# One accumulator in place of two for the first experts' scatter-add

## What is computed

```python
# T = 4096, K = 8, E = 64, CAP = 256, H = 256, F = 128
topk_idx, topk_w = _route(x, gate_weight, e_bias)            # 8 experts of each token, with weights
...
xe = jnp.zeros((E, CAP, H)).at[sorted_e, pos].set(tok_sorted, mode='drop')
h = silu(einsum('ech,efh->ecf', xe, w1)) * einsum('ech,efh->ecf', xe, w3)
ye = einsum('ecf,ehf->ech', h, w2)
...
out = segment_sum(vals * flat_w[:, None], flat_t, num_segments=T)
return out + shared
```

## Time and profile before

| | |
|---|---|
| three runs | 5909.79, 5924.18 (median), 5935.9 us |
| profiled execution, span | 5916.1 us (nothing is shown around it) |
| PE busy | 5058.1 us, 85% |
| DVE busy | 3390.4 us, 57% |
| ACT busy | 2567.7 us, 43% |
| POOL busy | 1828.3 us, 31% |
| first experts' phases, from the first gather to the last statistics | 235.6 to 693.0 and 2048.6 to 2506.0 us |

### The profile page before, as it was taken

How to read it: one execution, slowest core, us unless ns; L and a number is a source line. 1 busy time by engine, 2 the same in 40 slices (tenths; PEclk the granted TensorE clock), 3 DMA queues, 4 the chain that set the end, 5 groups by cost and what they waited for, 6 DMA issues and landing times. The chain is left out here.

```text
span 5916.1 us, 82750 instructions
## 1 busy us (share of the span) xinstructions
PE 5058.1 (85%) x29088; PEld 2711.9 (46%) x29088; DVE 3390.4 (57%) x6345; ACT 2567.7 (43%) x5102; POOL 1828.3 (31%) x1800
## 2 busy tenths in 40 slices
PE   6566489999978566499987999999999999799996
PEld 3455333333325455357973333333333333255896
DVE  7511468887846721241119788878888878343111
ACT  2311217776662311132215176766766766513221
POOL 2388311111101288534331122222222222104332
PEclk9778779999989687699998899999999999889998
DMA  3476561222213277606986411221221221120798
GB/s 107 116 148 149 138 171 33 62 58 68 62 53 104 76 156 151 149 26 212 330 269 198 108 37 40 63 49 40 64 47 40 64 48 40 55 69 1 267 318 268
DMA packets 503528, 659.28 MB, mean 111 GB/s; under 512 B 147310, under 2 KB 358318, under 8 KB 497998
## 3 DMA queue, kind: packets, MB, share of 16 engines
q1 hardware_dynamic: 370158, 500.99, 27.0%
q0 software_dynamic: 133056, 154.15, 13.2%
HBM read 489.33 MB, written 164.20 MB: 110 GB/s over the span
## 5 line engine op out<-in xcount | busy, mean ns | idle before, releaser
L1724 DVE TENSOR_REDUCE ea_mx<-ea_psA 128x1 f32<-128x512 f32 (+3 forms) x2304 | 1373.9, 653 | 242.0 <-PE ea_psA L1585 144.1
L1706 ACT ACTIVATE ea_pr<-ea_psB 128x512 f32<-128x512 f32 (+3 forms) x2560 | 1198.9, 535 | 567.4 <-PE ea_psB L1608 557.7
L1585 PE MATMUL ea_psA<-ex_kx,ex_qx 99*128 99x512 bf16 (+3 forms) x2560 | 868.4, 357 | 20.2 <-DVE ea_mx L1724 13.3
L1608 PE MATMUL ea_psB<-ex_qx,ex_kx 99*128 99x512 bf16 (+3 forms) x2560 | 846.2, 349 | 0.0
L1724 DVE TENSOR_REDUCE ba_mx<-ba_psA 128x1 f32<-128x512 f32 (+3 forms) x1152 | 686.2, 653 | 144.3 <-PE ba_psA L1585 95.6
L1706 ACT ACTIVATE ba_pr<-ba_psB 128x512 f32<-128x512 f32 (+3 forms) x1280 | 601.5, 536 | 288.9 <-PE ba_psB L1611 155.5
L1625 PE MATMUL ea_psO<-ea_pr,ea_vx 128*32 128x512 f32 (+3 forms) x5120 | 603.5, 543 | 20.9 <-POOL ea_pr L1554 14.0
L1585 PEld LDWEIGHTS ea_psA<-ex_kx,ex_qx 99*128 99x128 bf16 x2560 | 250.3, 98 | 551.8 <-DVE ea_mx L1724 427.8
L1585 PE MATMUL ba_psA<-bx_kx,bx_qx 108*128 108x512 bf16 (+3 forms) x1280 | 443.5, 364 | 7.8 <-PEq L1146 4.5
L1608 PE MATMUL ba_psB<-bx_qx,bx_kx 108*128 108x512 bf16 (+3 forms) x1280 | 424.9, 349 | 14.6 <-DMA bx_qx<-ba_mT 14.4
L1608 PEld LDWEIGHTS ea_psB<-ex_qx,ex_kx 99*128 99x128 bf16 x2560 | 246.5, 98 | 310.3 <-ACT ea_pr L1706 141.0
(11 more groups left out here) (528 smaller groups left out, 8260.9 us busy)
## 6 DMA issues: line engine op xcount, KB each, us to landing
de_wg<-in_L_rg SPq DMA_DIRECT2D x64, 512.0 KB, 4.7
de_wu<-in_L_ru SPq DMA_DIRECT2D x64, 512.0 KB, 5.9
de_wd<-in_L_rd SPq DMA_DIRECT2D x64, 512.0 KB, 7.3
fe_wg<-in_L_rg SPq DMA_DIRECT2D x64, 512.0 KB, 4.9
fe_wu<-in_L_ru SPq DMA_DIRECT2D x64, 512.0 KB, 5.9
fe_wd<-in_L_rd SPq DMA_DIRECT2D x64, 512.0 KB, 7.5
ae_w<-in_L_w SPq DMA_DIRECT2D x64, 384.0 KB, 3.6
ce_w<-in_L_w SPq DMA_DIRECT2D x64, 384.0 KB, 3.8
```

Source lines behind the costliest of these rows:

```text
L1585: last = nc.tensor.matmul(psA[:, slot, at:at + n], qx[0:KB, s, hh, t * P:(t + 1) * P], kx[0:KB, s, hh, k:k + n], start=True, stop=not diag)
L1608: last = nc.tensor.matmul(psB[:, slot, off:BLK], kx[0:KB, s, hh, kt * P:(kt + 1) * P], qx[0:KB, s, hh, Q * BLK + off:(Q + 1) * BLK], start ...
L1706: nc.scalar.activation(pr[:, j % 4, hh, off:BLK], psB[:, exp_slot(n), off:BLK], ACT.Exp).then_inc(s_exp, 1)
L1724: v.tensor_reduce(out, src, AX.X, ALU.max).then_inc(s_ar, 1)
```

## The change

There is one accumulator, `acc`, with 256 spare rows, and both halves are added to it. The kernel lets no two scatters that can share a row be in flight together: the two halves of one expert hold different tokens, so they still go out one behind the other, but both now wait for both halves of the expert before. Unused slots of even and odd columns get different spare rows, so that two halves in flight share none. `rows0`, `rows1` and `routed` have 256 spare rows too. The zero fill of the second accumulator, its load back and the add are gone.

```diff
+ROWS = T + 2 * P
...
 # norm_phase
-                    sp.dma_start(rows[DUMMY:DUMMY + P, :], zero[:, 0:width]).then_inc(s_zrow, 16)
+                    for a in range(2):
+                        sp.dma_start(rows[DUMMY + a * P:DUMMY + (a + 1) * P, :], zero[:, 0:width]).then_inc(s_zrow, 16)
...
 # slot_table
-    c.link(nc.vector.scalar_tensor_tensor(t1, t1, R["dummy"][:, 0:1], t2, ALU.subtract, ALU.mult))
-    c.link(nc.vector.tensor_scalar(idx, t1, R["dummy"][:, 0:1], None, ALU.add))
+    c.link(nc.vector.tensor_tensor(t1, t1, R["dummy"][:, 0:NCOL], ALU.subtract))
+    c.link(nc.vector.tensor_tensor(t1, t1, t2, ALU.mult))
+    c.link(nc.vector.tensor_tensor(idx, t1, R["dummy"][:, 0:NCOL], ALU.add))
...
 # route0_phase, SP
-                zsrc = zero[:].unsqueeze(1).broadcast_to((P, T * H // (P * 512), 512))
-                sp.dma_start(acc[1][0:T, :].rearrange("(p a) h -> p (a h)", p=P).rearrange("p (n f) -> p n f", f=512),
-                             zsrc).then_inc(s_zd, 16)
-                for a in acc:
-                    sp.dma_start(a[T:T + P, :], zero[:, 0:H]).then_inc(s_zd, 16)
+                for a in range(2):
+                    sp.dma_start(acc[DUMMY + a * P:DUMMY + (a + 1) * P, :], zero[:, 0:H]).then_inc(s_zd, 16)
...
-                sp.dma_start(acc[0][0:T, :].rearrange("(t p) h -> p t h", p=P),
+                sp.dma_start(acc[0:T, :].rearrange("(t p) h -> p t h", p=P),
...
 # experts0_phase, SP: the reload
-                    for buf, a in ((x, acc[0]), (x2, acc[1])):
-                        sp.dma_start(buf[:, q * (NT // NQ) * H:(q + 1) * (NT // NQ) * H].rearrange("p (t h) -> p t h", h=H),
-                                     a[q * (T // NQ):(q + 1) * (T // NQ), :].rearrange("(t p) h -> p t h", p=P)
-                                     ).then_inc(s_l[q], 16)
+                    sp.dma_start(x[:, q * (NT // NQ) * H:(q + 1) * (NT // NQ) * H].rearrange("p (t h) -> p t h", h=H),
+                                 acc[q * (T // NQ):(q + 1) * (T // NQ), :].rearrange("(t p) h -> p t h", p=P)
+                                 ).then_inc(s_l[q], 16)
...
 # experts0_phase, POOL: the scatters of expert n
+                    if n or run:
+                        for a in range(S0):
+                            pool.wait_ge(s_s[a], s0 + n * 16)
                     for a in range(S0):
-
-                        if n or run:
-                            pool.wait_ge(s_s[a], s0 + n * 16)
                         nc.gpsimd.indirect_dma_start(
-                            out=acc[a], out_offset=column(n, a), in_=y[:, n % RING, a, :], in_offset=None,
+                            out=acc, out_offset=column(n, a), in_=y[:, n % RING, a, :], in_offset=None,
...
 # experts0_phase, DVE: after the reload
-                    dve.wait_ge(s_l[q], 32)
-                    own = slice(q * (NT // NQ) * H, (q + 1) * (NT // NQ) * H)
-                    nc.vector.tensor_tensor(x[:, own], x[:, own], x2[:, own], ALU.add).then_inc(s_x, 1)
-                    dve.wait_ge(s_x, q + 1)
+                    dve.wait_ge(s_l[q], 16)
                     row_stats(nc, x, stats, range(q * (NT // NQ), (q + 1) * (NT // NQ)))
...
 # constants
-F32_CONSTS = (("ident", P), ("code", NT), ("dummy", 1), ("ecol1", E0), ("lower", NG0 * NG0), ("rev1", E1),
+F32_CONSTS = (("ident", P), ("code", NT), ("dummy", P), ("ecol1", E0), ("lower", NG0 * NG0), ("rev1", E1),
...
-        dummy=(DUMMY + p)[:, None], ecol1=row(np.arange(E0) * CAP + 1),
+        dummy=DUMMY + p[:, None] + P * (p[None, :] % 2), ecol1=row(np.arange(E0) * CAP + 1),
...
-    acc = [scratch(f"acc{a}", (T + P, H)) for a in range(S0)]
-    routed = scratch("routed", (T + P, H))
+    acc = scratch("acc", (ROWS, H))
+    routed = scratch("routed", (ROWS, H))
```

More of the change, by code:

```diff
@@ L195, in _ @@
                         sp.wait_ge(s_rows[u], 16 * (NB // 2))
-                    sp.wait_ge(s_zrow, 16)
+                    sp.wait_ge(s_zrow, 32)
                 if gate is not None:
@@ L550, in _ @@
                 sp.wait_ge(R["s_add"], NB)
-                sp.dma_start(acc[0][0:T, :].rearrange("(t p) h -> p t h", p=P),
+                sp.dma_start(acc[0:T, :].rearrange("(t p) h -> p t h", p=P),
                              x[:].rearrange("p (t h) -> p t h", h=H)).then_inc(s_acc, 16)
-                sp.wait_ge(s_zd, 48)
+                sp.wait_ge(s_zd, 32)
                 sp.wait_ge(s_wr, 16)
@@ L665, in experts0_phase @@
         y = sc.sb("y", [P, RING, S0, H])
-        x2 = sc.sb("x2", [P, NT * H])
         psX = sc.ps("psX", [P, 2, HC, CAP])
@@ L673, in experts0_phase @@
         s_xt, s_xe, s_h, s_sg, s_hh, s_y, s_yw = (sc.sem(n) for n in ("xt", "xe", "h", "sg", "hh", "y", "yw"))
-        s_x = sc.sem("x")
         s_l = [sc.sem(f"l{q}") for q in range(NQ)]
@@ L696, in _ @@
                 LEAD = RING - 1
-                bound = pool.to_reg(T + P - 1)
+                bound = pool.to_reg(ROWS - 1)
                 column = lambda n, a: bass.IndirectOffsetOnAxis(ap=idx[:, n * S0 + a:n * S0 + a + 1], axis=0)
@@ L2094, in macaron_kernel @@
     scratch = lambda n, s, dt=F32: nc.dram_tensor(n, s, dt, kind="Internal").ap()
-    rows0, rows1 = scratch("rows0", (T + P, ROW0)), scratch("rows1", (T + P, ROW1))
-    acc = [scratch(f"acc{a}", (T + P, H)) for a in range(S0)]
-    routed = scratch("routed", (T + P, H))
+    rows0, rows1 = scratch("rows0", (ROWS, ROW0)), scratch("rows1", (ROWS, ROW1))
+    acc = scratch("acc", (ROWS, H))
+    routed = scratch("routed", (ROWS, H))
     lv = [scratch(f"lv{i}", (3, B * H, S), BF16) for i in range(4)]
```

## The result

| | before | after |
|---|---|---|
| median of 18 runs each | 5920.39 us (5903.85 to 5939.61) | 5945.56 us (5935.25 to 5958.28) |
| ratio | | 1.0045, 95% interval 1.0035 to 1.0055 |
| profiled execution, span | 5916.1 us | 5933.4 us |

The changed kernel is slower by 0.45%: by the ratio 20.7 to 32.6 us. That is under the 0.5% which the prediction took as the least that can be told, but with 18 runs of each kernel the interval lies clear of no change. The 25 us are the rest of terms of which the largest is nearly 30, so the parts are what is worth reading.

The account below looks back on a forecast made before the run. POOL, issuing DMAs one behind another, bounds the first-expert phases. +20.0 steady wait, +21.4 tail, -28.0 reload and +1.3 slot tables sum to +14.7, so 5930.8 by the span and 5939 us with 8.1 for the median; range 5916 to 5972.

Parts of the forecast that it names:

- Steady wait: First-expert phases while gathers remain: a first half also waits for the previous expert's second half; 10.0 us a phase, +20.0.
- The shift: Steady part: POOL's wait delays the next first half, so weight loads already set off come earlier against it; 18 becomes 10.0 us a phase.
- the term's threshold: Steady part: a second half landing within 4.63 - 0.71 = 3.92 us is free; each later one costs the difference.
- Tail: Last experts of each phase, without gathers: six steps of 6.31 us instead of 4.53, 10.7 us a phase, +21.4.
- Reload: Loading x back after each phase: four loads and statistics, 17.6 us in place of 31.70 and 31.50, saving 28.0.
- Slot table: Slot tables, which POOL waits for: three linked DVE steps instead of two, 0.39 or 0.27 us each, four tables, +1.3.
- Costed at nothing: Accumulator zero fill, second zero block of rows, wider constant, register bounds and fewer POOL waits: 0 us.
- the slower one: Steady part: weight loads stay on second halves, 34.3 us of wait in place of 20.0; +29.0, 5953 us; chance 0.23.
- the bad stretch: Steady part: a pair's first load issued 1.9 to 3.2 us after a first half's start makes the second half land late.
- a lock: Steady part: the rhythm locks weight loads onto the bad place, raising the wait to 80 us, 5999 us; chance 0.07.
- The case without steady wait: Steady part: weight loads settle on gathers and first halves, so the wait vanishes; -5.3, 5919 us; chance 0.15.
- the wait that does nothing: Steady part and tail stay as they are, leaving only reload and slot tables; -26.7, 5897 us; chance 0.05.

Follow-up runs that it names:

- e2: The kernel before without the second accumulator's reload and its add, leaving the second halves' results out of x: 5889.24 us, ratio 0.9949.
- e6: The kernel before, waiting for both halves only in experts 58 to 63 and the second phase's first expert: 5938.22 us, ratio 1.0043.
- e7: The kernel before with 256 spare rows everywhere, the wider constant and the three-step slot table, two accumulators and their own waits kept: 5929.25 us, ratio 1.0014.
- e3: The changed kernel with weight loads set off by the second half's scatter landing eight experts back, not PE's down projection: 5929.70 us, 1.0012 against the kernel before.
- e10: The changed kernel with weight loads set off by the landing of gathers that POOL issues before the first half: 5970.38 us, 1.0081 against the kernel before.
- e8: The changed kernel with both zero blocks of the norm phases written after the row writes, not ahead: 5948.47 us, ratio 1.0042 to the kernel before.
- e1: The kernel before, two accumulators kept, with each scatter waiting for both halves of the expert before: 5967.97 us, ratio 1.0080.

## Why the prediction was right

The time, 5945.56, lies 6.6 us above the forecast and inside its range, and the case came out that was called likeliest: a change under 0.5%, on the slow side. The change itself is further off: 25.2 us between the medians, 14.7 in the sum. 3.8 us of that difference do not show in the time, because the forecast stands on the median of three runs, and that of 18 is 3.8 us lower; this part is luck. By its steps:

- **Steady wait: right in mechanism, a little small.** Predicted 10.0 a phase, measured 14.1 and 10.6. The shift is there: counted as in the prediction, by landings later than 3.92 us, the 55 late second halves of the trace before (34.3 us) became 37 late ones with 18.4 us in all, near the 20.0 predicted. The loads show it too: in 24 experts the first load behind a first half came 1.9 to 3.2 us after it, and now in 12. But the 34.3 came from one execution. In e2, e6 and e7, which have no steady wait either, 40 to 42 second halves are late, by 24.6 to 26.2 us, so the shift took off less than the prediction reckoned, and the near match with 20.0 is partly luck. Mis-sized was the term's threshold: in the steady part POOL goes on 0.81 to 0.83 us after a landing, not 0.71 as taken from the earlier trace rows, so a landing is free up to some 3.82 us. 41 waits by 0.1 are 4.1 us. In four of the 41 POOL goes on only 1.1 to 1.5 us after the landing, another 2.0 us, and why is open; 18.4 + 4.1 + 2.0 is 24.5 of the 24.7. e3 shows the load's place to be the cause of most of it, and e10 that loads brought nearer make it larger.
- **Tail: right.** 6.31 us a step predicted, 6.37 and 6.31 measured; alone in e6.
- **Reload: right.** 17.6 us predicted from the start of the kernel, 17.1 and 17.3 measured; alone in e2. The first statistics follow each other at (700.17 - 691.23) / 3 = 2.98 us for 1 MB, the 350 GB/s of the earlier trace rows. By the 425 GB/s that the Trainium skill's page "DMA: Bandwidth & Descriptors" (section Bandwidth) gives for 16 MB, an estimate of the saving would have been smaller by 4.2 us over both phases. These loads of 1 MB do not reach that rate.
- **Slot table: too dear.** The three steps follow each other at 0.32 us, not 0.39, and the tables of the first experts end 0.27 us later each. Those of the second experts are not waited for: their first gather came 43 us after the table in the kernel before. +0.5 in place of +1.3.
- **Costed at nothing: the step that failed.** "The second zero block of rows is one more SP issue ahead of writes that wait for DVE" looked at SP's queue and not at the DMAs behind it. DVE waits for the landing of the first write, and that landing comes 1.3 us later. It cost 3.6 us between the two profiles, 5.4 by the means of the table in e8. The prediction's own test, that nothing outside the phases should move by several microseconds, points to the place. The rest of that paragraph stood: the first scatter starts at 253.89, 254.55 before, so neither the wider constant nor the missing zero fill shows.

Of the rivals, the slower one was near: the measured steady mean is 24.7 / 114 = 0.22 us an expert, its price starts at 0.306, and the measured interval ends at 32.6 us, above the bound of 29.6. The shift, which took loads out of the bad stretch, kept away from it, but it was not needed: with the late landings of e2, e6 and e7, and POOL's later start on 41 waits, I estimate 32 us, 0.28 an expert. In e10, where the loads were sent close ahead of the second halves, the mean was 38.8 / 114 = 0.34, just over that price and half of the 80 / 114 = 0.70 of a lock; a lock itself was not tried. The case without steady wait needs an edit of the load's trigger (e3), and the wait that does nothing was refuted by the first tail step.

What stays open: what is left of the steady wait in e3; why the steady wait differs between the phases (14.1 and 10.6, in e1 14.9 and 12.5); 3 us between the sum of terms and the difference of the medians, which the interval covers; and whether a zero fill for a second accumulator costs anything when put back, which was not tried by itself.

## What to carry to other kernels

Merging two buffers saves the work on the second one but ties their writers into one chain: price the chain where nothing covers it (here six steps of 1.8 us in each tail against 14 us of reload) before the saving is counted. A wait that is usually free is decided by whichever transfer collides with the landing it waits for; moving that transfer's trigger can take back most of the wait (18.7 of 24.7 us here). One more DMA may be called free only after looking at who waits for the DMAs behind it, and at what stands ahead of it.

## What the runs showed that was not expected

- Behind three weight loads of 512 KB, two writes of 128 spare rows (128.5 KB each) ahead of a series of writes delay the first of these by 1.3 us more than one does (landing 7.2 against 5.9 us), though SP issues it at the same distance from the stage's start. With none ahead, DVE's wait for it is 3.3 us instead of 4.9 and 6.2. Behind three loads of 256 KB, in the first experts' norms, the first write lands after 3.0 us with one block or two (160 KB each) before and after the change. That the size of the loads makes the difference was not tried by itself.
- POOL goes on 0.74 us after the landing in the tails of the kernel before (the prediction's 0.71 came from a landing rounded to 3.7), and 0.77 in the tails with two waits, in the changed kernel as in e1 and e6: the second wait is some 0.03 us. In the steady part it is 0.81 to 0.83 for most waits, and why is open.
- Transfers whose trigger hangs on the engine that they delay move out of its way: in e10, for each microsecond that POOL had waited, the load came about a microsecond earlier against the next scatter.
